# Layer 3 top-32 attention: the last replacing pass of one head of two is given up, and the kept keys of that head are marked by ranks that TensorE counts and ScalarE takes

## The chip, the cores and the metric

One Trainium2 chip, one of its cores. The metric is the device time of one launch in microseconds, the median of the runs. In the views PE is TensorE, DVE is VectorE, ACT is ScalarE, POOL is GpSimd.

## The reference, cut to what matters

The kernel computes a four-layer decoder on 8 sequences of 256 tokens with 128 features. The change is in the attention of layer 3, with a smaller edit in that of layer 2. Layer 3 has 16 heads of 8 features, and each query keeps only its 32 largest scores (`K = 32`):

```python
def _L3_attn_ref(x, Wq, bq, Wk, bk, Wv, bv, Wo, bo):
    ...
        top_s, top_i = jax.lax.top_k(scores, kk)
    ...
```

The scores are `q k^T / sqrt(8)` (256 by 256 per head and sequence), the kept ones go through a softmax, all others count as nothing, and the result is mixed with the values and projected by `Wo`. Of equal scores at the border the one at the lower position is kept.

## The kernel before

**The stage.** `topk_attention` works on 64 groups (`GROUPS`). A group is two heads of one sequence, cut in four units (`U = 4`) of 128 queries by 256 keys: units 0 and 1 are the first head, units 2 and 3 the second. The scores of a group fill two PSUM banks, and group n + 2 uses those of group n. Each engine runs an order written out by hand, a loop over t, and waits on semaphores that count.

- `score` (PE, L3719): four FP32 matmuls with 32 rows (a head is padded to 32), the two heads at two different row groups of the array. It waits until ScalarE has read the banks (`probs_ready` of group n - 2).
- `choose` (DVE, L3885 and L3888): four rounds. A round is four MAX8 (eight largest of each query) and four MATCH_REPLACE8 (puts -3e38 in their places in `raw`). After round four the 32 largest are gone from `raw`. The last instruction gives `scores_max`.
- `soften` (ACT, L3821 to L3829): the negated maximum as bias, the sum over the 32 kept ones (`few`), then for each unit the exponential of all scores (`probs`) and that of `raw` (`rest`).
- `pick` (POOL, L3936, L3938): `probs - rest` leaves the kept ones; then times the inverse of the sum.
- `turn` (PE, L3765): eight FP32 transposes; `take_turned` (ACT, L3838) copies them out of PSUM; `mix` (PE, L3742) multiplies with the values.
- On even t PE also runs `project` (L3706, L3707: keys and queries of the next tile, which is two groups), and ACT takes them in `take_queries` (L3811, L3812). On odd t ACT takes the mixed heads in `take_heads` (L3846), which waits for `mix`. Every eighth group `put_out` multiplies with `Wo`. In the first 16 steps keys and values of the next sublayer are made in between (`project_context`).

So in step t ScalarE softens group t - 1 and then copies the turned group t - 2, while VectorE works on group t.

**The layer 2 stage.** `delta_outputs` has 16 units. For each, PE makes the scores of four bands of 32 rows (L2670, L2673) in four banks, DVE multiplies all of them by a mask in one instruction (L2749, 1536 columns) and PE mixes (L2688, L2691). The banks are single, so the scores of a unit wait for the mask of the one ahead.

Of the kernel before, what the change touches and what calls it, by code (L numbers as in the profile page):

```python
# [11 lines left out]
ALU = mybir.AluOpType  # L12
# [2609 lines left out]
def delta_outputs(c, k, q_odd, q_even, U, padded, masks, probs, oT, inv_q, gates, vt, o_t, squares, sums):  # L2622
# [27 lines left out]
    with nc.Block() as block:  # L2650
        @block.tensor
        def _(pe):
# [11 lines left out]
            def score(n):  # L2664
                b, e = units[n]
                src = (q_even, q_odd)[e]
                if n >= 1:
                    pe.wait_ge(c.scores_masked.sem, c.scores_masked.at(n))
                for j in range(4):
                    nc.tensor.matmul(scores(j)[:, 0:3:2, :], k[band[j], b * S:b * S + P], src[band[j], b * S:(b + 1) * S],  # L2670
                                     start=True, stop=True, tile_position=(32 * j, 0))
                for j in range(4):
                    mm = nc.tensor.matmul(scores(j)[:, 1, :], k[band[j], b * S + P:(b + 1) * S],  # L2673
                                          src[band[j], b * S + P:(b + 1) * S], start=True, stop=True,
                                          tile_position=(32 * j, 0))
                mm.then_inc(c.scores_ready.sem, 1)

            def mix(n):
                b, e = units[n]
                pe.wait_ge(c.scores_masked.sem, c.scores_masked.at(n + 1))  # L2680
# [60 lines left out]
        def _(dve):  # L2741
            v = nc.vector
            for n in range(len(units) + 5):
                if n < len(units):
                    b, e = units[n]
                    dve.wait_ge(c.scores_ready.sem, c.scores_ready.at(n + 1))
                    if n >= 2:
                        dve.wait_ge(c.mixed_ready.sem, c.mixed_ready.at(n - 1))
                    v.tensor_tensor(probs[n % 2], c.psum[:, 0:4, 0:3 * P].rearrange("p j (a x) -> p j a x", x=P),  # L2749
                                    masks[:, b % 4].unsqueeze(1).broadcast_to([P, 4, 3, P]), ALU.mult) \  # L2750
                        .then_inc(c.scores_masked.sem, 1)
# [20 lines left out]
    for s, n in ((c.updates_moved, 4), (c.updates_placed, 4), (c.scores_ready, len(units)), (c.scores_masked, len(units)),  # L2772
# [878 lines left out]
def topk_attention(c):  # L3651
# [6 lines left out]
    NG, GROUPS, TILES = H // 2, B * H // 2, B * H // 4  # L3658
    a = Arena(c)
# [6 lines left out]
    top8, few = a.take(2, U, K // 8, 8), a.take(2, U, K)  # L3666
    values = c.T[:, 0, :].rearrange("p (t f) -> p t f", f=P)
# [11 lines left out]
    def held(tile):  # L3679
        return bank(6)[:, tile % 2 * S:(tile % 2 + 1) * S]  # L3680
# [14 lines left out]
    with nc.Block() as block:  # L3695
        @block.tensor
        def _(pe):
# [12 lines left out]
            def score(n):  # L3710
                tile = n // 2
                if n % 2 == 0:
                    pe.wait_ge(c.qk_taken.sem, c.qk_taken.at(tile + 1))
                if n >= 2:
# [921 lines left out]
```

## Time and profile before

| | |
|---|---|
| runs | 2515.19 us median of 3 (2509.85 to 2515.55) |
| profiled execution | 2510.24 us, span 2508.4 us |
| busy share of the span | PE 75%, DVE 69%, ACT 45%, POOL 28% |
| mean granted clock of PE | 0.812 of full speed |
| layer 3 attention stage | about 1526 to 2296 us of the span |

### The profile page before, as it was taken

How to read it: one execution, taken by the hardware profiler on the slowest of the kernel's cores; microseconds unless marked ns; L12 is line 12 of the kernel's file. 1: busy time of each engine (PE TensorE's matmuls, PEld its weight loads, DVE VectorE, ACT ScalarE, POOL GpSimd, SP SyncE). 2: the span in 40 equal slices, each digit the busy share in tenths (PEclk: the TensorE clock that was granted, in tenths of full speed). 3: DMA queues.
4: the chain of work that ended last, by engine and by line, in shares of the span. 5: the costliest groups of instructions: out<-in, count | busy, mean ns of one | idle time of the engine just before them, and what ended most of it. 6: DMA issues, size and time to landing. Idle time of an engine off the chain costs nothing. (4 is left out here: it accounts for less than half of the span.)

```text
span 2508.4 us, 36866 instructions
## 1 busy us (share of the span) xinstructions
PE 1871.5 (75%) x11751; PEld 1113.4 (44%) x11763; DVE 1736.4 (69%) x5543; ACT 1134.2 (45%) x3143; POOL 711.7 (28%) x620
## 2 busy tenths in 40 slices
PE   6996889853877999979997875565555555555778
PEld 2654447442445666644464553343333333333443
DVE  4236342267765666657746777999999999995655
ACT  3653442251315777731233654555555555454411
POOL 1200045014432333310032411444433433332130
PEclk8997899965998999989998896666666566566979
DMA  5000001400000000000200000000000000000000
GB/s 212 2 1 1 27 27 29 151 14 1 2 2 1 2 2 1 0 1 0 94 2 1 1 1 1 1 1 1 1 1 1 1 1 1 1 1 1 1 1 17
DMA packets 10591, 37.76 MB, mean 15 GB/s; under 512 B 1344, under 2 KB 7488, under 8 KB 9136
## 3 DMA queue, kind: packets, MB, share of 16 engines
q1 hardware_dynamic: 8880, 33.04, 3.4%
q0 software_dynamic: 1536, 2.59, 0.4%
q8 instruction: 85, 1.39, 0.2%
q14 instruction: 90, 0.74, 0.1%
HBM read 30.15 MB, written 5.51 MB: 14 GB/s over the span
## 5 line engine op out<-in xcount | busy, mean ns | idle before, releaser
L3719 PE MATMUL psum<-work 32*128 32x256 f32 x512 | 130.5, 654 | 291.8 <-ACT work L3829 291.8
L3888 DVE MATCH_REPLACE8 work<-work 128x256 f32<-128x256 f32 x768 | 304.8, 405 | 0.0
L3936 POOL TENSOR_TENSOR work<-work 128x1024 f32<-128x1024 f32 x64 | 150.6, 2354 | 494.5 <-ACT work L3829 494.5
L3885 DVE MAX8 work<-work 128x8 f32<-128x256 f32 x768 | 266.1, 406 | 0.0
L3719 PEld LDWEIGHTS psum<-work 32*128 32x128 f32 x512 | 77.6, 311 | 318.2 <-ACT work L3829 161.8
L709 POOL TENSOR_TENSOR work<-work 128x256 f32<-128x256 f32 (+2 forms) x144 | 133.3, 944 | 225.9 <-DVE work L997 225.9
L925 ACT ACTIVATE work<-work 128x128 f32<-128x128 f32 (+1 forms) x320 | 144.9, 454 | 19.1 <-DVE work L972 17.3
L3829 ACT ACTIVATE work<-work 128x256 f32<-128x256 f32 x256 | 128.4, 502 | 0.0
L3742 PE MATMUL psum<-work,tiles 128*8 128x256 f32 x512 | 117.2, 610 | 13.6 <-ACT work L3838 13.6
L3938 POOL TENSOR_TENSOR work<-work 128x1024 f32<-128x1024 f32 x64 | 121.1, 1892 | 6.2 <-DVE work L3910 1.2
L3827 ACT ACTIVATE work<-psum,work 128x256 f32<-128x256 f32 x256 | 117.4, 459 | 0.0
L3765 PE MATMUL psum<-small_weights,work 128*128 128x128 f32 x512 | 100.8, 362 | 15.6 <-POOL work L3938 15.6
L3765 PEld LDWEIGHTS psum<-small_weights,work 128*128 128x128 f32 x512 | 83.5, 191 | 61.9 <-POOL work L3938 42.5
L352 DVE RECIPROCAL work<-work 128x128 f32<-128x128 f32 x36 | 34.3, 952 | 107.2 <-ACT work L424 106.9
L3888 DVE MATCH_REPLACE8 work<-work,psum 128x256 f32<-128x256 f32 x256 | 102.8, 411 | 0.0
L966 DVE CUSTOM_DVE_ANT_0 work<-psum,work 128x128 f32<-128x128 f32 (+1 forms) x320 | 99.6, 367 | 2.8
L3885 DVE MAX8 work<-psum 128x8 f32<-128x256 f32 x256 | 90.5, 413 | 7.7 <-PE psum L3719 5.8
L891 ACT ACTIVATE work<-psum,big_weights 128x256 f32<-128x256 f32 x128 | 57.9, 473 | 76.3 <-PE psum L773 75.7
L2209 DVE TENSOR_TENSOR work<-work,psum 128x320 f32<-128x320 f32 (+1 forms) x56 | 32.0, 573 | 74.7 <-PE psum L2047 66.0
L1285 ACT ACTIVATE work<-psum 128x1024 f32<-128x1024 f32 x64 | 62.0, 1021 | 42.2 <-PE psum L1192 42.2
L273 PE MATMUL psum<-residual,small_weights 128*128 128x512 f32 x96 | 56.4, 719 | 31.7 <-PEq L169 17.8
L3823 ACT ACTIVATE work<-work 128x32 f32<-128x32 f32 x256 | 79.0, 310 | 2.1
(616 smaller groups left out, 4629.3 us busy)
## 6 DMA issues: line engine op xcount, KB each, us to landing
big_weights<-L0f_dram SPq DMA_DIRECT2D x1, 6117.5 KB, 29.3
big_weights<-L_dram SPq DMA_DIRECT2D x1, 5772.0 KB, 17.5
big_weights<-L_dram SPq DMA_DIRECT2D x1, 4952.5 KB, 15.8
choice_rows<-tiles SPq DMA_DIRECT2D x2, 1024.0 KB, 10.5
tiles<-choice_rows SPq DMA_DIRECT2D x8, 256.0 KB, 5.0
big_weights<-L_dram SPq DMA_DIRECT2D x1, 2027.0 KB, 20.2
big_weights<-L_dram SPq DMA_DIRECT2D x1, 1630.5 KB, 13.8
big_weights<-L0f_dram SPq DMA_DIRECT2D x1, 1630.5 KB, 6.4
```

The lines of the kernel that those rows point to most:

```text
L709: ins = nc.gpsimd.tensor_tensor(part, part, rsum[:, g % 4, q:U:U // n].unsqueeze(2) .broadcast_to([P, n, seen(q)]), ALU.mult)
L925: ins = nc.scalar.activation(probs[:, g % 2, u, 0:seen(u)], src, ACT.Exp, bias=nbias[:, g % 2, u:u + 1], scale=scale, accum_out=sums[:, g ...
L966: ins = nc.vector.tensor_tensor_reduce(raw[:, s, u, 0:seen(u)], scores(g)[:, u, 0:seen(u)], mask(mb, u % 2)[:, 0:seen(u)], 1.0, NEG, ALU.a ...
L3719: mm = nc.tensor.matmul(scores(n)[:, u, :], qb[head, tile % 2, u % 2 * P:(u % 2 + 1) * P], kb[head, tile % 2, :], start=True, stop=True, t ...
L3742: mm = nc.tensor.matmul(held(tile)[at:at + D, :], values[:, 2 * b + kt, lo:lo + D], turned[:, n % 2, head, kt, :], start=(kt == 0), stop=( ...
L3765: mm = nc.tensor.transpose(bank(4 + head)[:, at:at + P], probs[:, n % 2, 2 * head + q, kt * P:(kt + 1) * P], ident)
L3827: nc.scalar.activation(probs[:, s, u, :], scores(n)[:, u, :], ACT.Exp, bias=nbias[:, s, u:u + 1], scale=SCALE)
L3829: ins = nc.scalar.activation(rest[:, s, u, :], raw[:, s, u, :], ACT.Exp, bias=nbias[:, s, u:u + 1], scale=SCALE)
L3885: ch.step(v.max(top8[:, n % 2, u, r, :], src[:, u, :]))
L3888: ins = v.match_replace(raw[:, n % 2, u, :], top8[:, n % 2, u, r, :], src[:, u, :], REPLACED)
L3936: ch.link(g.tensor_tensor(mine, mine, rest[:, n % 2], ALU.subtract))
L3938: g.tensor_tensor(mine, mine, rsum[:, n % 2, :].unsqueeze(2).broadcast_to([P, U, S]), ALU.mult) \
```

## The change

For each group but the last (`FINAL` = 63) the units 2 and 3 (`M = 2`, one head) are marked in another way:

- VectorE leaves out the last two MATCH_REPLACE8 of round four.
- ScalarE writes `sign(threshold - score)` of these units as bf16, with a sum (`balance`), ahead of `few`; it leaves out two exponentials of `raw`. Then it squares the turned signs (`square`), and takes the ranks from PSUM (`keep_ranks`), and only then copies the turned probabilities of the group in front.
- TensorE turns the signs (`turn_signs`), and adds up seven bf16 matmuls in the score banks of units 2 and 3 (`rank`). The score matmuls of group t + 1 come in two halves: head one ahead of `rank`, head two behind it (and behind `project`), since its banks must have been read by `keep_ranks`.
- GpSimd subtracts 512 columns instead of 1024, clamps the ranks between 0 and 1 and multiplies units 2 and 3 by them.
- `held` has one buffer instead of two (the other half of bank 6 holds the turned signs).

The last group keeps the old marking, but VectorE does the subtraction and the scaling unit by unit, copies one of the two turned heads, and adds the last output itself; three quarters of the last `put_out` go ahead, and ScalarE copies the turned group 62 ahead of softening group 63. In `delta_outputs` scores and mask go in halves of two bands.

```diff
@@ delta_outputs
-                for j in range(4):
-                    nc.tensor.matmul(scores(j)[:, 0:3:2, :], k[band[j], b * S:b * S + P], src[band[j], b * S:(b + 1) * S],
...
+                for half in range(2):
+                    if n >= 1:
+                        pe.wait_ge(c.scores_masked.sem, c.scores_masked.at(2 * n - 1 + half))
+                    for j in (2 * half, 2 * half + 1):
...
@@ topk_attention, tensor
+            def turn_signs(n):
+                pe.wait_ge(signs_ready.sem, signs_ready.at(n + 1))
...
+                for kt in range(2):
+                    for u in range(M):
+                        mm = nc.tensor.transpose(signs_t[:, kt, u, :], signs_by_unit[:, u, kt * P:(kt + 1) * P], ident16)
+                mm.then_inc(signs_turned.sem, 1)
+
+            def rank(n):
+                pe.wait_ge(squares_kept.sem, squares_kept.at(n + 1))
+                order = scores(n)[:, U - M:U, :]
+                nc.tensor.matmul(order.rearrange("p u k -> p (u k)"), far, signs, start=True, stop=False)
+                for u in range(M):
+                    nc.tensor.matmul(order[:, u, :], one_row[0:1, :], place_row[0:1, :], start=False, stop=False)
+                    for kt in range(2):
+                        mm = nc.tensor.matmul(order[:, u, :], squares[:, kt, u, :], prefix[:, kt, :], start=False,
+                                              stop=(kt == 1 and u == M - 1))
+                mm.then_inc(ranks_ready.sem, 1)
...
             for t in range(GROUPS + 3):
+                if 0 <= t - 1 < FINAL:
+                    turn_signs(t - 1)
                 if t + 1 < GROUPS:
-                    score(t + 1)
+                    score(t + 1, 0, U - M)
+                if 0 <= t - 1 < FINAL:
+                    rank(t - 1)
                 if t % 2 == 0 and t // 2 + 1 < TILES:
                     project(t // 2 + 1)
+                if t + 1 < GROUPS:
+                    score(t + 1, U - M, U)
...
@@ topk_attention, scalar
+                    signed = nc.scalar.activation(signs_by_unit[:, m, :], scores(n)[:, u, :], ACT.Sign, scale=-1.0,
+                                                  bias=top8[:, s, u, LAST, 7:8], accum_out=balance[:, s, m:m + 1])
...
+            def square(n):
+                act.wait_ge(signs_turned.sem, signs_turned.at(n + 1))
...
+            def keep_ranks(n):
+                act.wait_ge(ranks_ready.sem, ranks_ready.at(n + 1))
...
+                for u in range(M):
+                    ins = nc.scalar.activation(ranks[:, u, :], scores(n)[:, U - M + u, :], ACT.Relu, scale=2.0,
+                                               bias=balance[:, n % 2, u:u + 1])
+                ins.then_inc(ranks_kept.sem, 1)
...
+                if t == GROUPS:
+                    take_turned(t - 2)
                 if 0 <= t - 1 < GROUPS:
                     soften(t - 1)
-                if 0 <= t - 2 < GROUPS:
+                if 0 <= t - 1 < FINAL:
+                    square(t - 1)
+                if 0 <= t - 1 < FINAL:
+                    keep_ranks(t - 1)
+                if 0 <= t - 2 < GROUPS and t != GROUPS:
                     take_turned(t - 2)
...
@@ topk_attention, vector
+                replaced = U - M if r == LAST and n < FINAL else U
...
-                for u in range(U):
+                for u in range(replaced):
...
@@ topk_attention, gpsimd
-                ch.link(g.tensor_tensor(mine, mine, rest[:, n % 2], ALU.subtract))
+                ch.link(g.tensor_tensor(first, first, rest[:, n % 2, 0:U - M], ALU.subtract))
+                pool.wait_ge(ranks_kept.sem, ranks_kept.at(n + 1))
+                ch.link(g.tensor_scalar(ranks, ranks, 1.0, 0.0, ALU.min, ALU.max))
+                ch.link(g.tensor_tensor(marked, marked, ranks, ALU.mult))
```

TensorE's order, one even step in the middle of the stage (the semaphores in brackets are what the first of a row waits for). Before:

```order
L3765 MATMUL psum<-small_weights,work 128x128 [waits turned_copied,probs_picked]
L3765 MATMUL psum<-small_weights,work 128x128 x7
L3719 MATMUL psum<-work 128x256 [waits probs_ready]
L3719 MATMUL psum<-work 128x256 x3
L3706 MATMUL psum<-normed_input,big_weights 128x256 [waits qk_taken]
L3707 MATMUL psum<-normed_input,big_weights 128x256
L3742 MATMUL psum<-work,tiles 8x256 [waits out_copied,turned_copied]
L3742 MATMUL psum<-work,tiles 8x256 x3
```

The same step in the changed kernel (`aux_s` is `signs_ready`, `aux_s2` is `squares_kept`, `aux_s3` is `ranks_kept`):

```order
L3806 MATMUL psum<-small_weights,work 128x128 x7
L3747 MATMUL psum<-work 128x128 [waits aux_s]
L3747 MATMUL psum<-work 128x128 x3
L3735 MATMUL psum<-work 128x256 [waits probs_ready]
L3735 MATMUL psum<-work 128x256
L3753 MATMUL psum<-work 128x512 [waits aux_s2]
L3755 MATMUL psum<-work 128x256
L3757 MATMUL psum<-work 128x256 x2
L3720 MATMUL psum<-normed_input,big_weights 128x256 [waits qk_taken]
L3721 MATMUL psum<-normed_input,big_weights 128x256
L3735 MATMUL psum<-work 128x256 [waits aux_s3]
L3782 MATMUL psum<-work,tiles 8x256 [waits out_copied,turned_copied]
```

The four score matmuls no longer stand together: seven rank matmuls (L3753, and L3755 with two L3757 twice), the projection and a wait for ScalarE stand between the first head and the second.

ScalarE's order in an odd step, before and then in the changed kernel (`aux_pe` is `signs_turned`, `aux_pe2` is `ranks_ready`):

```order
L3827 ACTIVATE work<-psum,work 128x256
L3829 ACTIVATE work<-work 128x256
L3838 COPY work<-psum 128x512 [waits mixed_ready,probs_turned]
L3838 COPY work<-psum 128x512
L3821 ACTIVATE work<-work 128x4 [waits probs_turned,sums_inverted,scores_max]
```

```order
L3873 ACTIVATE work<-work 128x4 [waits probs_turned,sums_inverted,scores_max]
L3877 ACTIVATE work<-psum,work 128x256 x2
L3883 ACTIVATE work<-work 128x32 x3
L3887 ACTIVATE work<-psum,work 128x256 x4
L3892 ACTIVATE work<-work 128x256 x2
L3899 ACTIVATE work<-psum 128x512 [waits aux_pe]
L3908 ACTIVATE work<-psum,work 128x256 [waits probs_picked,aux_s,aux_pe2]
L3917 COPY work<-psum 128x512 [waits mixed_ready,probs_turned]
L3925 COPY work<-psum 128x256 [waits mixed_ready]
```

Between the exponentials and the copy of the turned probabilities ScalarE now has two places at which it waits for TensorE (L3899, L3908), and everything behind them waits too.

## Rows read from the trace of the kernel before

**Rows 1.** Windows: the attention stage, then two stretches of one group.

```profile
core 0: us, PE busy (x) PEld busy (x) DVE busy (x) ACT busy (x) POOL busy (x), PEclk, DMA share, GB/s
1526.00:2276.00 750.00, 429.79 (x1754) 243.31 (x1750) 747.01 (x3138) 393.00 (x1304) 286.53 (x145) 0.63 0.00 1
1908.10:1915.20 7.10, 7.10 (x26) 4.04 (x27) 7.10 (x32) 1.73 (x4) 4.25 (x2) 0.50 0.00 1
1915.20:1918.60 3.40, 0.42 (x4) 0.18 (x2) 3.40 (x15) 3.20 (x14) 0.00 (x0) 1.00 0.00 0
```

**Rows 2.** Two waits of the stage: total, times, longest.

```profile
PE psum L3719 <- ACT work L3829: 291.8, 62, 6.4
...
DVE work L3885 <- PE psum L3719: 5.8, 1, 5.8
```

**Rows 3.** Timeline of one group: start, time, engine, line.

```profile
1903.45 0.21 ACT L3821 ACTIVATE work<-work 128x4 f32<-128x4 f32 x1 [2.57 <-DVE work L3888]
1903.62 1.42 DVE L3885 MAX8 work<-psum 128x8 f32<-128x256 f32 x4 [0.20 <-DVE work L3888]
...
1904.92 0.45 ACT L3827 ACTIVATE work<-psum,work 128x256 f32<-128x256 f32 x1
...
1905.02 0.41 DVE L3888 MATCH_REPLACE8 work<-work,psum 128x256 f32<-128x256 f32 x1
1905.28 0.50 ACT L3829 ACTIVATE work<-work 128x256 f32<-128x256 f32 x1
...
1905.42 0.41 DVE L3888 MATCH_REPLACE8 work<-work,psum 128x256 f32<-128x256 f32 x1
...
1907.94 1.06 ACT L3838 COPY work<-psum 128x512 f32<-128x512 f32 x2
...
1908.10 2.08 PE L3719 MATMUL psum<-work 32*128 32x256 f32 x8 [5.25 <-ACT work L3829]
...
1910.11 1.22 PE L3706 MATMUL psum<-normed_input,big_weights 128*128 128x256 f32 x2
1910.56 1.89 POOL L3938 TENSOR_TENSOR work<-work 128x1024 f32<-128x1024 f32 x1
...
1912.12 1.88 PE L3742 MATMUL psum<-work,tiles 128*8 128x256 f32 x8
1912.22 0.47 ACT L3811 ACTIVATE work<-psum,big_weights 128x256 f32<-128x256 f32 x1 [3.23 <-PE psum L3707]
...
1915.25 1.08 DVE L3885 MAX8 work<-psum 128x8 f32<-128x256 f32 x3
```

**Rows 4.** Source view of L288: two row groups together, then one alone.

```profile
L288 PE MATMUL psum<-work,small_weights x8: 270/270/372, 1515.5 to 1516.0; 32*128 32x128 f32 x8
...
L288 PE MATMUL psum<-work,small_weights x4: 270/270/372, 1516.7 to 1517.2; 32*128 32x128 f32 x4
```

**Rows 5.** Nearest rows for added operations, grouped by form.

```profile
L4333 PE MATMUL psum<-work,small_weights 128*128 128x512 bf16 x30 | 11.2, 380 | 1.2 <-PEq L1575 1.2
...
L3954 POOL TENSOR_TENSOR tiles<-tiles,big_weights 128x512 f32<-128x512 f32 x4 | 5.1, 1270 | 0.3
...
L3166 POOL TENSOR_SCALAR tiles<-tiles 128x2048 f32<-128x2048 f32 x1 | 2.2, 2212 | 0.1
```

**Rows 6.** Timeline of two units of the layer 2 stage.

```profile
727.43 0.71 PE L2670 MATMUL psum<-tiles 32*128 32x256 f32 x8 [0.72 <-DVE work L2749]
...
728.44 1.76 DVE L2749 TENSOR_TENSOR tiles<-psum,work 128x1536 f32<-128x1536 f32 x1 [0.73 <-PE psum L2673]
...
730.25 0.71 PE L2670 MATMUL psum<-tiles 32*128 32x256 f32 x8 [1.09 <-DVE tiles L2749]
```

**Rows 7.** Timeline of the end of the attention stage.

```profile
2276.66 0.21 ACT L3821 ACTIVATE work<-work 128x4 f32<-128x4 f32 x1 [3.72 <-DVE work L3888]
...
2285.72 1.97 PE L3765 MATMUL psum<-small_weights,work 128*128 128x128 f32 x8 [1.57 <-POOL work L3938]
...
2295.19 0.72 POOL L3944 TENSOR_TENSOR residual<-residual,work 128x256 f32<-128x256 f32 x1 [9.53 <-remote]
```

More of the change, by code:

```diff
@@ L3666, in topk_attention @@
     top8, few = a.take(2, U, K // 8, 8), a.take(2, U, K)
+    M, LAST = U // 2, K // 8 - 1
+    signs, squares = (a.take(M * S // 2).bitcast(BF16) for _ in range(2))
+    signs_by_unit = signs.rearrange("p (u k) -> p u k", u=M)
+    squares = squares.rearrange("p (t u q) -> p t u q", t=2, u=M)
+    ranks, balance = a.take(M, S), a.take(2, M)
+    ident16, far, place_row, one_row = (a.take(n // 2).bitcast(BF16) for n in (P, P, S, P))
+    prefix = a.take(2, S // 2).bitcast(BF16)
+    strict = a.take(P)
+    signs_ready, signs_turned, squares_kept, ranks_ready, ranks_kept = c.aux_s, c.aux_pe, c.aux_s2, c.aux_pe2, c.aux_s3
     values = c.T[:, 0, :].rearrange("p (t f) -> p t f", f=P)
@@ L3708, in project, with score @@
                     .then_inc(c.qk_ready.sem, 1)
-            def score(n):
+            def score(n, lo_unit, hi_unit):
                 tile = n // 2
-                if n % 2 == 0:
+                if n % 2 == 0 and lo_unit == 0:
                     pe.wait_ge(c.qk_taken.sem, c.qk_taken.at(tile + 1))
-                if n >= 2:
+                if n >= 2 and lo_unit == 0:
                     pe.wait_ge(c.probs_ready.sem, c.probs_ready.at(n - 1))
-                for u in range(U):
+                if n >= 2 and hi_unit == U:
+                    pe.wait_ge(ranks_kept.sem, ranks_kept.at(n - 1))
+                for u in range(lo_unit, hi_unit):
                     lo = (n % 2 * 2 + u // 2) * 32
@@ L3766, in turn @@
                                                      probs[:, n % 2, 2 * head + q, kt * P:(kt + 1) * P], ident)
+                    if n == FINAL and head == 0:
+                        mm.then_inc(c.probs_turned.sem, 1)
+                        pe.wait_ge(c.probs_picked.sem, c.probs_picked.at(n + 2))
                 mm.then_inc(c.probs_turned.sem, 1)
@@ L3783, in _ @@
             make_values(0)
-            score(0)
+            score(0, 0, U)
             make_values(1)
@@ L3836, in take_turned @@
                     act.wait_ge(c.mixed_ready.sem, c.mixed_ready.at(n - 1))
-                for head in range(2):
+                for head in range(1 if n == FINAL else 2):
                     ins = nc.scalar.copy(turned[:, n % 2, head].rearrange("p t s -> p (t s)"), bank(4 + head))
@@ L3954, in mask_context, with tables @@
                     ch.link(g.tensor_tensor(x, x, c.w("L3x_vmask").unsqueeze(1).broadcast_to([P, CH // P, P]), ALU.mult))
-            for t in range(GROUPS + 4):
-                if 0 <= t - 1 < GROUPS:
+            def tables():
+                g.tensor_copy(ident16, ident)
+                g.tensor_scalar(far, ident, -512.0, 0.0, ALU.mult, ALU.add)
+                g.tensor_scalar(place_row, c.w("position"), -1.0, float(K), ALU.mult, ALU.add)
+                g.memset(one_row, 1.0)
+                g.memset(prefix[:, 0, P:], 0.5)
+                g.memset(prefix[:, 1, 0:P], -0.5)
+                ch.link(g.tensor_tensor(strict, c.w("upper"), ident, ALU.subtract))
+                ch.step(g.tensor_scalar(prefix[:, 0, 0:P], strict, 1.0, -0.5, ALU.mult, ALU.add))
+                ch.link(g.tensor_scalar(prefix[:, 1, P:], strict, 1.0, -0.5, ALU.mult, ALU.add))
+                g.memset(strict, 0.0).then_inc(c.tables_ready.sem, 1)
+            tables()
+            for t in range(GROUPS + 3):
+                if 0 <= t - 1 < FINAL:
                     pick(t - 1)
```

114 lines of the change are left out of this document (79 added, 35 removed).

## The prediction

> **What bounds the kernel now.** I first read the windows of the attention stage [rows 1]. It holds 750 of the 2508 us of the span, and VectorE is busy for 747.0 of them. PE is busy for 430 us at a mean granted clock of 0.63, ScalarE for 393, GpSimd for 287. The waits say the same: PE waits 291.8 us for ScalarE's last exponential in 62 places, which costs nothing, while VectorE waits for scores once, 5.8 us at the start [rows 2]. Then I read the timeline of one group [rows 3]. VectorE starts it at 1903.62 and the next one at 1915.25, so a group takes 11.63 us. ScalarE begins to soften at 1903.45, 0.03 us after VectorE's last record. PE gets the score banks at 1908.10 and has the new scores in them 2.08 us later, at 1910.18, more than 5 us before VectorE asks for them at 1915.25. The stage is VectorE's alone, and whatever shortens a group there shortens the stage, as long as the circle from VectorE through ScalarE and PE back to VectorE, and ScalarE's own row of work, stay under the new length of a group.
>
> **What is removed.** Two MATCH_REPLACE8 in 63 groups. They start 0.40 apart (1905.02, 1905.42), a little less on the mean of a round, so I take 0.395 each [rows 3]. A group of VectorE becomes 11.63 - 0.79 = 10.84 us. 63 x 0.79 = 50 us is the ceiling of this part.
>
> **What is added on ScalarE.** Offsets are from the start of softening. The bias copy and the four sums take 1.47 us (1903.45 to 1904.92). An exponential from PSUM starts 0.36 before its neighbour (1904.92 to 1905.28); all eight take 3.02 (to 1907.94), which leaves 0.395 for one from SBUF [rows 3]. Sign with a sum isn't in the trace: at least 0.36, at most the 0.45 of the record and a read of the sum behind it, some 0.65. A sum of 32 columns costs 0.31 ((1.47 - 0.24)/4), about 0.1 over a plain one, so I take 0.46, and 0.92 for both, of which the wait behind the bias copy hides 0.1. Sums end at 2.3, four exponentials at 3.75, two at 4.55, with the last record's tail `probs_ready` comes at 4.65. Before, it came at 4.65 too (1908.10). The square is a 512-column read of PSUM like the copies (1.06 for two): 0.53, done at 5.1, behind the score matmuls and so hidden.
>
> **What is added on PE, and the price of cutting the scores in two.** Rank is 2048 columns of bf16 (512 and six times 256). The nearest row is 512 columns in 380 ns at full clock, 11.2 us busy for 30 [rows 5]. Some 0.17 of it is the way of the last column through the array, and 0.21 its own; at half clock I take 0.43, so rank is 1.7 plus 0.16 for the first weights and 0.2 for the last column, 2.07 us; at full clock about 1.05. If bf16 cost what FP32 does (0.5 for a record of 256 columns, half of the 2.01 us from 1910.11 to 1912.12 over two records each [rows 3]), it would be 4. The four transposes of signs are 512 columns, 0.6 or 0.35.
>
> The part that the diff hides is `score`. L288 multiplies FP32 with 32 rows in one row group of the array. Eight records at two row groups stand between 1515.5 and 1516.0, and four records at one row group between 1516.7 and 1517.2, with the same durations [rows 4]. So two row groups run side by side, and half the matmuls at one row group take as long. The scores before have exactly this form, two heads at two row groups, 8 records in 2.08 us. Cut by head, each half takes the whole 2.0 us at half clock (1.0 at full), and PE pays the scores twice: +2.0 per group, and 1.0 of it stands ahead of rank, where it would otherwise be.
> The Trainium skill, TensorEngine Tiling, "Theoretical Speedup", allows up to 4x for a contraction of 32 rows, one array tile beside the other. By it a lone head could use a quarter of the array, and the trace agrees in kind: two tiles gave 2x, and one gives nothing. Without such packing the cut would cost nothing, and the sums below would be 1.0 us shorter at each half.
>
> **At which clock.** PE is granted 0.50 for the 7.10 us in which it is busy without a gap, and 1.00 for the 3.40 us behind, when it has almost nothing to do [rows 1]. The mean of 0.63 is 74% of the time at half speed. So I work the step out for both.
>
> Half clock, even step: `probs_ready` 4.65; first head 4.70 to 6.71; rank to 8.8; ScalarE takes the ranks, 0.82 for two (0.36 and a record of 0.46), to 9.7; the copy of the turned group, 1.06, to 10.7. PE projects from 8.6 to 10.7, ScalarE takes the queries, 0.85 (1912.22, two records of 0.47 overlapping), to 11.6. Second head 10.6 to 12.7, mix 1.88 [rows 3] to 14.5, turn 1.97 [rows 7] to 16.5, signs of the next group 17.0; they should be there at 4.65 of the next step, 16.3: 0.7 late.
> Odd step: ranks taken 9.7, copy 10.7, second head 9.7 to 11.7, mix to 13.6, and the heads are taken behind it, 0.4 (256 columns from PSUM, like an exponential): 14.0.
> A pair takes 11.6 + 0.7 + 14.0 = 26.3 us, 13.15 per group, bound by ScalarE that waits for PE.
> Full clock: first head 5.7, rank 6.8, ranks taken 7.6, copy 8.7; even: queries 9.6; odd: second head 8.7, mix 9.8, heads 10.2. Both are under 10.84, and VectorE stays the bound.
>
> The new loop through GpSimd is near that too: ranks taken, clamp, two multiplications (1.27 for 512 columns [rows 5], 1.89 for 1024 [rows 3]), turn, signs, first head, rank, ranks. The clamp isn't there; GpSimd's only comparable row is 2.21 for 2048 columns [rows 5], a quarter of it 0.55, so between 0.55 and 2.21, and I take 0.66. With 0.2 for the three links this is 4.0 + 2.0 + 0.5 + 2.0 + 2.1 + 0.9 = 11.5 at half clock and 8.5 at full.
>
> **The sum.** What stays open is the mix of the clocks. PE gets more to do (7.1 us of work per step become some 11.5 at half clock), which speaks for more time at full speed than now; but two heads one after the other fill less of the array, and 7.10 us of gapless work weren't enough before. I take 65% at half: 10.84 + 0.65 x (13.15 - 10.84) = 12.34, that is +0.71 against 11.63, and 63 x 0.71 = +45 us.
> The tail: from 2276.66 to the last GpSimd record's end at 2295.91 are 19.25 us [rows 7]. After: softening starts 2 to 4 us later, because the turned group 62 is copied first; then 4.6 to the last exponential, 1.3 for VectorE's last two pieces, 1.0 for four transposes, 0.6 copy, 1.9 mix, 0.4 heads, 0.7 for one product of four, 0.45 for the addition: 13 to 15. So -5.
> `delta_outputs`: a unit takes 2.82 us (727.43 to 730.25), 1.01 for scores and 1.76 for the mask [rows 6]. Its scores run at four row groups at once, so half of them takes as long as all, and PE's work per unit becomes 0.9 + 0.9 + 0.8 for the mix + 0.2 = 2.8 less what the halves still overlap; VectorE's floor is about 2.2. Between 0 and -0.6 for 16 units, I take -0.2: -3.
> Total +45 - 5 - 3 = +37 on the profiled execution's own 2510.2, 2547. That execution lies 5 us under the median of 2515.2 and beside the lowest run, so I put the median after at 2550.
>
> **The rivals.**
> 1. *VectorE stays the bound (faster).* If PE is at full speed nearly all through the stage, each group is 10.84: -50 - 5 - 3 = -58, 2455. For it: PE would be busy in almost every stretch of a half-clock step, and the stretches of pauseless work get longer. It decides at the share of half clock where 10.84 + s x 2.31 = 11.63 + 8/63, s = 0.40; below that the kernel is faster. Against it: at full clock PE pauses from about 2.3 to 4.7 of each step. The Trainium skill, TensorE: Matmul & The Clock Gate, "What's actually happening", says that sustained work brings 2.4 GHz and idleness 1.2; [rows 1] shows the rise only at 1915.20, when the step's work was over. Chance 0.20.
> 2. *PE stays at half clock.* 13.15 per group, +96 - 8 = +88, 2600 and a little more, if the clamp is at its upper bound too. Chance 0.17.
> 3. *The two balance,* near s = 0.40, no difference: 0.08. A mild gain between it and the first: 0.05.
> 4. The forecast, a mix: 0.50.
>
> **How the numbers follow.** Slower 0.67 (4 and 2), within 0.3% 0.08, faster 0.25; 0.3% is about 8 us, roughly what this measurement can tell. The range leaves out the lower half of the first rival's cases and the far end of the second: 2462 to 2618. The forecast's own range is 2522 to 2588 (s from 0.45 to 0.9).
>
> **What would show it.** The two halves of `score` at 2.0 us each at clock 0.50; VectorE idle ahead of its first MAX8 of a group, released by PE's second half, or ScalarE's softening later than 0.03 us behind VectorE's last record; ScalarE waiting at L3899 and L3908 for some 3 us a group. It is wrong if VectorE is busy for nearly all of the stage after too, or if the halves of `score` take 1 us at half clock, or if PE is granted over 0.85 in the mean.

## The result and the profile after

The changed kernel takes 2582.28 us (median of 4 runs, 2581.62 to 2599.37) against 2515.37 for the kernel before: a ratio of 1.0293 (95% interval 1.0274 to 1.0312), 2.9% slower. The medians alone give 1.027; the ratio weighs all executions, 2599.4 us among them, but that of experiment e4 leaves out its slow one, 2605.6 us. The direction was forecast, the size was not: by medians +35 us forecast, +67 measured.

The page of the kernel after, busy time by engine, over its profiled span of 2580.0 us:

```profile
PE 2094.7 (81%) x12412; PEld 1231.4 (48%) x12456; DVE 1696.7 (66%) x5317; ACT 1212.2 (47%) x3456; POOL 759.2 (29%) x753
```

Its windows view of the attention stage, columns as in [rows 1], and the waits of that stretch (engine and line, released by; total, times, longest, in us):

```profile
1526.00:2330.00 804.00, 628.31 (x2319) 346.74 (x2349) 675.49 (x2776) 457.54 (x1569) 325.23 (x266) 0.64 0.00 1
```

```profile
POOL work L4038 <- ACT work L3892: 260.5, 58, 12.6
POOL work L4040 <- ACT work L3908: 207.8, 61, 4.4
ACT work L3908 <- PE psum L3757: 187.2, 61, 4.0
DVE work L3971 <- PE psum L3735: 114.2, 43, 5.2
PE psum L3735 <- ACT work L3892: 101.1, 40, 3.1
...
ACT work L3925 <- PE psum L3782: 76.7, 29, 3.0
```

VectorE, busy 747 of 750 us before [rows 1], is now busy 675 of 804 and stands 114 us ahead of its first MAX8, released by the second part of the scores; before that was 5.8 us, once [rows 2]. PE went from 430 us of 750 to 628 of 804, at the same mean clock, 0.64 for 0.63.

The stage's first and last group, by VectorE's first MAX8:

```profile
1522.92 0.76 DVE L3971 MAX8 work<-psum 128x8 f32<-128x256 f32 x2 [6.15 <-PE psum L3735]
...
2344.42 0.76 DVE L3971 MAX8 work<-psum 128x8 f32<-128x256 f32 x2 [1.91 <-PE psum L3735]
```

821.5 us for 63 groups; the same two starts in the trace before lie 738.3 apart. So the span's +71.6 us (2508.4 to 2580.0) are: +83.2 in the groups, -3.7 ahead of them, -5.8 in the tail up to the next stage's first matmul, and -2.1 behind. Ahead of them lies `delta_outputs`: from its first score matmul to the end of its last mask it takes 40.7 us for 45.9. Everything that went wrong is in the groups. Two steps of them, PE and ScalarE alone, even step first:

```profile
1903.50 2.07 PE L3735 MATMUL psum<-work 32*128 32x256 f32 x4 [2.34 <-ACT work L3892]
1905.51 0.61 PE L3753 MATMUL psum<-work 128*128 128x512 bf16 x1
...
1907.62 1.06 PE L3720 MATMUL psum<-normed_input,big_weights 128*128 128x256 f32 x2
1907.87 0.84 ACT L3908 ACTIVATE work<-psum,work 128x256 f32<-128x256 f32 x2 [3.94 <-PE psum L3757]
...
1909.47 2.07 PE L3735 MATMUL psum<-work 32*128 32x256 f32 x4
1910.30 0.21 ACT L3873 ACTIVATE work<-work 128x4 f32<-128x4 f32 x1
1911.47 1.88 PE L3782 MATMUL psum<-work,tiles 128*8 128x256 f32 x8
...
1915.46 1.12 PE L3735 MATMUL psum<-work 32*128 32x256 f32 x4
...
1918.90 2.07 PE L3735 MATMUL psum<-work 32*128 32x256 f32 x4 [0.93 <-ACT work L3908]
```

Each head's scores, x4 records, take 2.07 us at clock 0.50; before, both heads, x8, took 2.08 [rows 3]. Of these parts the one at 1915.46 alone is at full speed (1.12). ScalarE stands 3.94 us for the ranks. And once in eight groups there is a step that the forecast has no sum for:

```profile
1880.29 1.88 PE L3782 MATMUL psum<-work,tiles 128*8 128x256 f32 x8
1882.10 3.16 PE L3791 MATMUL psum<-work,big_weights 128*128 128x256 f32 x8
1885.10 1.04 PE L3806 MATMUL psum<-small_weights,work 128*128 128x128 f32 x8
...
1885.30 0.47 ACT L3931 ACTIVATE work<-psum,big_weights 128x256 f32<-128x256 f32 x1 [6.07 <-PE psum L3791]
1885.68 0.20 ACT L3873 ACTIVATE work<-work 128x4 f32<-128x4 f32 x1
...
1890.38 1.11 PE L3735 MATMUL psum<-work 32*128 32x256 f32 x4 [3.14 <-ACT work L3892]
...
1894.68 2.07 PE L3735 MATMUL psum<-work 32*128 32x256 f32 x4 [0.93 <-ACT work L3908]
```

```profile
1896.79 1.09 DVE L3971 MAX8 work<-psum 128x8 f32<-128x256 f32 x3 [3.63 <-PE psum L3735]
```

ScalarE stands 6.07 us for the output product (L3931). The softening behind it starts at 1885.68, PE stands 3.14 us for it, and VectorE gets its next scores at 1896.79, 16.4 us after the last ones. Seven groups have such a step, every eighth from the 12th on: the first takes 16.5 us, the other six 16.4 each.

### The profile page after: what moved, and what is told of

Its sections match the earlier page's. It is cut to its first block and busy times, and to the rows that moved or that the text cites. A ratio compares the mean times of both kernels' runs of the same rounds, so it can differ in the third digit from the quotient of the medians.

```text
span 2580.0 us, 38569 instructions
## 1 busy us (share of the span) xinstructions
PE 2094.7 (81%) x12412; PEld 1231.4 (48%) x12456; DVE 1696.7 (66%) x5317; ACT 1212.2 (47%) x3456; POOL 759.2 (29%) x753
## 5 line engine op out<-in xcount | busy, mean ns | idle before, releaser
L3735 PE MATMUL psum<-work 32*128 32x256 f32 x512 | 216.5, 566 | 133.1 <-ACT work L3892 103.4
L3974 DVE MATCH_REPLACE8 work<-work 128x256 f32<-128x256 f32 x642 | 255.5, 407 | 0.0
L3735 PEld LDWEIGHTS psum<-work 32*128 32x128 f32 x512 | 122.1, 265 | 194.1 <-ACT work L3892 85.0
L4038 POOL TENSOR_TENSOR work<-work 128x512 f32<-128x512 f32 x63 | 79.8, 1267 | 266.9 <-ACT work L3892 266.7
L3908 ACT ACTIVATE work<-psum,work 128x256 f32<-128x256 f32 x126 | 52.8, 470 | 192.7 <-PE psum L3757 192.7
L3806 PE MATMUL psum<-small_weights,work 128*128 128x128 f32 x512 | 111.8, 391 | 25.8 <-POOL work L4043 24.2
L3806 PEld LDWEIGHTS psum<-small_weights,work 128*128 128x128 f32 x512 | 92.3, 207 | 70.2 <-POOL work L4043 65.0
L4043 POOL TENSOR_TENSOR work<-work 128x1024 f32<-128x1024 f32 x63 | 119.2, 1892 | 4.9
L3782 PE MATMUL psum<-work,tiles 128*8 128x256 f32 x512 | 109.5, 575 | 3.9 <-ACT work L3917 3.1
L4040 POOL TENSOR_SCALAR work<-work 128x512 f32<-128x512 f32 x63 | 38.6, 612 | 214.8 <-ACT work L3908 214.8
L3887 ACT ACTIVATE work<-psum,work 128x256 f32<-128x256 f32 x256 | 99.6, 477 | 0.0
L4041 POOL TENSOR_TENSOR work<-work 128x512 f32<-128x512 f32 x63 | 79.8, 1266 | 5.3
```

The source lines that it names most:

```text
L3735: mm = nc.tensor.matmul(scores(n)[:, u, :], qb[head, tile % 2, u % 2 * P:(u % 2 + 1) * P], kb[head, tile % 2, :], start=True, stop=True, t ...
L3782: mm = nc.tensor.matmul(held[at:at + D, :], values[:, 2 * b + kt, lo:lo + D], turned[:, n % 2, head, kt, :], start=(kt == 0), stop=(kt == ...
L3806: mm = nc.tensor.transpose(bank(4 + head)[:, at:at + P], probs[:, n % 2, 2 * head + q, kt * P:(kt + 1) * P], ident)
L3887: nc.scalar.activation(probs[:, s, u, :], scores(n)[:, u, :], ACT.Exp, bias=nbias[:, s, u:u + 1], scale=SCALE)
L3974: ins = v.match_replace(raw[:, n % 2, u, :], top8[:, n % 2, u, r, :], src[:, u, :], REPLACED)
L4038: ch.link(g.tensor_tensor(first, first, rest[:, n % 2, 0:U - M], ALU.subtract))
```

## Experiments

Every ratio is to the kernel before, run on the same chip. That kernel's median was 2515.4 us beside the kernel after, 2516.3 for e1 to e4, 2522.8 for e5 to e8, 2522.9 for e9 to e12 and 2514.2 for e13 and e14, so between these sets the ratios are to be compared and not the times; a difference of 0.0100 is 25 us. Group lengths are from VectorE's first MAX8 to the next group's, the mean of 62 without the first. The clock is the windows view's PEclk over 1560 to 2200 us, with PE's busy time in these 640 us. For the kernel before that is 373 us at 0.64, with groups of 11.66.

| kernel | us | ratio (95%) | group | PE busy | PEclk |
|---|---|---|---|---|---|
| after | 2582.3 | 1.0293 (1.0274 to 1.0312) | 13.02 | 502 | 0.65 |
| e1 no ranks | 2503.4 | 0.9942 (0.9920 to 0.9964) | 11.66 | 371 | 0.63 |
| e8 two less | 2459.4 | 0.9757 (0.9719 to 0.9794) | 10.87 | 395 | 0.64 |
| e2 whole scores | 2536.4 | 1.0081 (1.0053 to 1.0110) | 12.11 | 453 | 0.67 |
| e3 side by side | 2505.8 | 0.9957 (0.9933 to 0.9981) | 11.60 | 445 | 0.68 |
| e6 copy first | 2593.2 | 1.0295 (1.0237 to 1.0353) | 13.11 | 507 | 0.64 |
| e4 output later | 2574.5 | 1.0220 (1.0188 to 1.0253) | 12.68 | 511 | 0.65 |
| e5 three edits | 2494.6 | 0.9898 (0.9864 to 0.9933) | 11.36 | 435 | 0.71 |
| e7 filler | 2473.7 | 0.9816 (0.9775 to 0.9857) | 11.08 | 475 | 0.82 |
| e9 three + filler | 2471.2 | 0.9802 (0.9772 to 0.9833) | 10.95 | 473 | 0.81 |
| e10 filler, after | 2563.9 | 1.0172 (1.0141 to 1.0202) | 12.48 | 537 | 0.74 |
| e11 filler, before | 2518.9 | 0.9991 (0.9975 to 1.0008) | 11.66 | 406 | 0.72 |
| e12 short extras | 2580.7 | 1.0235 (1.0202 to 1.0267) | 12.78 | 517 | 0.61 |
| e13 output last | 2556.8 | 1.0171 (1.0137 to 1.0205) | 12.46 | 519 | 0.64 |
| e14 all last | 2465.7 | 0.9810 (0.9793 to 0.9827) | 10.92 | 477 | 0.82 |

**The parts priced alone.** e1 is the kernel after with the marking by ranks undone:

```
-                    score(t + 1, 0, U - M)
+                    score(t + 1, 0, U)
-                if 0 <= t - 1 < FINAL:
-                    rank(t - 1)
...
-                replaced = U - M if r == LAST and n < FINAL else U
+                replaced = U
```

> The tail and the halved units of delta_outputs as in the kernel after, the attention groups as in the kernel before (all 16 MATCH_REPLACE8, scores in one piece, no signs and no ranks). My forecast priced these two edits at -5 and -3 us. Theory: the whole loss is in the groups, so this is 8 to 9.5 us under the kernel before, 2506 us, and the groups take 11.67 us again. Rival: the edits around the groups hold a part of the loss that the two traces hide from each other; then the time is 2515 us or more.

e8 is e1 with the `replaced` line of the kernel after.

> The kernel without ranks (tail and delta units as after, scores in one piece, 2503.4 us), with the last two MATCH_REPLACE8 of a group left out and nothing in their place: the second head of each group keeps its 25th to 32nd largest in what is subtracted, so its probabilities are not the reference's. It prices the removal alone. Forecast: 63 x 0.79 = 50 us, groups of 10.84 us, 2454 us. Rival: the chain through ScalarE and PE doesn't fit into 10.84 us at half clock even without ranks, and groups end at 11.2 or more, 2475 us.

e1 gave 2503.4, groups of 11.66: the loss lies in the marking alone, and the edits around it bring 9 to 20 us by the interval, where the traces of before and after show 9.5 and the forecast had 8. e8 gave 2459.4; it leaves the second head's marking unfinished, so it is a price and no kernel to use. The two MATCH_REPLACE8 are worth 0.0185, 47 us, and 0.79 us a group, as forecast. Without ranks the chain fits into the shorter group at a mean clock of 0.64.

**The cut of the scores.** e2 puts the scores back in one piece, behind rank:

```
-                if t + 1 < GROUPS:
-                    score(t + 1, 0, U - M)
                 if 0 <= t - 1 < FINAL:
                     rank(t - 1)
...
-                    score(t + 1, U - M, U)
+                    score(t + 1, 0, U)
```

> The kernel after, with the four score matmuls of a group in one piece behind the rank matmuls (and behind the projection in even steps), so that the two row groups run side by side again. Theory A (the cut costs PE the scores twice, half of it ahead of the rank matmuls): rank starts up to 2.0 us earlier in a step, the scores take 2.08 us where the second half took 2.07, and a group gets 0.8 us shorter on the mean, 12.2 us, some 2530 us. The group that takes 16.4 us once in eight stays. Rival B (the cut is cheap, the chain through GpSimd and the late turned copy hold the step): no change that can be told, 2575 to 2585 us, VectorE still idle 114 us before its first MAX8.

e3 keeps the cut but makes it across the heads, one half of the queries of both in each piece:

```
+    def slot(u):
+        return 2 * (u % 2) + u // 2
...
-                    lo = (n % 2 * 2 + u // 2) * 32
+                    lo = (n % 2 * 2 + u % 2) * 32
...
-                    mm = nc.tensor.matmul(scores(n)[:, u, :], qb[head, tile % 2, u % 2 * P:(u % 2 + 1) * P],
+                    mm = nc.tensor.matmul(scores(n)[:, slot(u), :], qb[head, tile % 2, u // 2 * P:(u // 2 + 1) * P],
...
-                order = scores(n)[:, U - M:U, :]
-                nc.tensor.matmul(order.rearrange("p u k -> p (u k)"), far, signs, start=True, stop=False)
                 for u in range(M):
-                    nc.tensor.matmul(order[:, u, :], one_row[0:1, :], place_row[0:1, :], start=False, stop=False)
+                    own = scores(n)[:, slot(U - M + u), :]
+                    nc.tensor.matmul(own, far, signs_by_unit[:, u, :], start=True, stop=False)
+                    nc.tensor.matmul(own, one_row, place_row, start=False, stop=False)
...
```

> The kernel after, with another cut: each piece of the scores holds one half of the queries of both heads, so its two matmuls lie in different row groups and different banks. The marked units are the second halves of the queries. The first rank matmul becomes two of 256 columns, and the one of one row has 128 rows of which 127 are zero. Theory A (what costs is that a piece has one row group): a piece takes 1.05 us at half clock instead of 2.07; with one piece ahead of rank and one behind, a group gets up to 2 us shorter where PE bounds it, to about 11.8 on the mean, some 2505 us. Rival B (the chain through GpSimd and ScalarE's order hold the step): 0.3 us per group at most, 2560 us. Rival C (with fewer busy columns the clock stays at 0.50 longer): the pieces get short but the mean clock falls under 0.62 and the time stays over 2530 us.

By ratios e2 takes 53 us off the kernel after and e3 85, or 35 and 66 off e4 below, which has the same order of instructions as the kernel after. Both are as theory A had them, and rival B is out; so is e3's rival C, with a mean clock of 0.68. e3's timeline, two pieces at half clock and full:

```profile
1909.64 1.22 PE L3738 MATMUL psum<-work 32*128 32x256 f32 x4 [2.03 <-ACT work L3894]
...
1914.28 0.70 PE L3738 MATMUL psum<-work 32*128 32x256 f32 x4
```

The same x4 records with the same columns take 1.22 where the kernel after pays 2.07. e3 gives back about all of the 67 us that the kernel after lost, though it changes two other things with the cut: the first rank matmul comes in two, and the one of one row has 128 rows. e2 changes nothing but the cut and the place of the scores. The Trainium skill, TensorEngine Tiling (Array Packing), "Theoretical Speedup", gives up to 4x for a dimension of 32. The traces bear out that there is something to gain, and show a condition that decides here: a piece must hold work for more than one row group. In e3 the two matmuls of a piece start 0.01 us apart, in the kernel after one follows the other. They need not alternate in the code: the kernel before gives both matmuls of one head and then both of the other, and the four take 2.08 us [rows 3].

**ScalarE's order.** e6 and e4 each change one thing in ScalarE's program of the kernel after, e5 changes both in e3:

```
+                if 0 <= t - 2 < GROUPS and t != GROUPS:
+                    take_turned(t - 2)
                 if 0 <= t - 1 < FINAL:
                     keep_ranks(t - 1)
-                if 0 <= t - 2 < GROUPS and t != GROUPS:
-                    take_turned(t - 2)
```

> The kernel after with one move on ScalarE: the copies of the turned probabilities go ahead of the ranks. In the kernel after, ScalarE stands 3.1 us at the ranks in each step. Theory A (the cut scores make PE the bound, it has no gap behind the rank matmuls in even steps): at half clock the copy ends before rank does, so ranks are kept at the same time and the mix is no longer behind the copy; but PE takes up the second piece as before and a group changes by under 0.3 us: 2565 to 2585 us. Rival B (ScalarE's order costs the time): at least 0.8 us per group less, 2530 us or lower.

```
             for t in range(GROUPS + 4):
+                if t >= 11 and (t - 11) % NG == 0 and t < GROUPS + 3:
+                    take_output((t - 11) // NG)
...
-                if t >= 10 and (t - 10) % NG == 0 and t < GROUPS + 2:
-                    take_output((t - 10) // NG)
```

> The kernel after, with ScalarE's taking of the output product moved from the end of its step to the start of the next one. Theory: the group of 16.4 us once in eight comes from ScalarE standing at that wait (up to 6.3 us) while the next softening is due; without it these groups take 13 us, 7 x 3.4 = 24 us less, some 2557 us. Rival: PE is late in these steps by the product itself, and ScalarE waits elsewhere for the same time: the groups of 16 us stay and the time is 2575 us or more.

> The kernel with pieces of the scores side by side (2505.8 us), and two moves on ScalarE as well: the turned probabilities of the group in front are copied ahead of the ranks, and the output product is taken at the start of the next step. In that kernel a group takes 11.6 us on the mean against a floor of 10.84, 14 of 62 are over 12, and once in eight it is 13.2. Theory A (what is left is ScalarE standing at the ranks, 2.5 us a group, with the copy and so the mix behind it): the copy goes into that wait, groups come to 11.1 on the mean, 2475 us. Rival B (what is left is PE at the half clock, whatever ScalarE's order): ranks come later by the copy's 1.0 us, the second piece with them, and the time stays between 2495 and 2510 us.

e6: no difference from the kernel after (1.0295 and 1.0293). Although ScalarE stands 187 us at the ranks, its order isn't what costs. e4 doesn't do what was meant: between the end of step t and the start of the next one ScalarE has nothing else in those steps, so the order of instructions is the same as in the kernel after on every engine. It says nothing on the product, and is a second measurement of the kernel after's order: 1.0220 (1.0188 to 1.0253) for 1.0293 (1.0274 to 1.0312), 18 us apart. Its trace has 800.4 us for the 63 groups, for 821.5. The two traces agree within 0.1 us a group up to the 12th; from the 36th on e4's groups with the product take 14.4 us for 16.4. Windows of one such group, in the kernel after and in e4:

```profile
2085.26:2101.64 16.38, 11.14 (x44) 6.20 (x43) 11.02 (x45) 7.21 (x25) 4.36 (x4) 0.71 0.01 2
```

```profile
2077.44:2091.85 14.41, 9.17 (x44) 5.29 (x43) 10.93 (x45) 7.22 (x25) 5.38 (x5) 0.81 0.01 2
```

The same 44 instructions of PE, at 0.81 for 0.71, are busy 2 us less. Whether the build, the chip or the execution decides which of the two rhythms a run falls into isn't shown. Below, less than 0.0073 (18 us) between two kernels with PE as the bound is not read as an effect. e5, which so is e3 with the copy first, lies 15 us under e3 by ratios (11 by medians), within that bound and nearer to rival B.

**The clock.** e7 is e3 with work whose product nobody reads:

```
+            def fill():
+                for _ in range(10):
+                    nc.tensor.matmul(bank(4)[:, 0:S], ident16, prefix[:, 0, :], start=True, stop=True)
...
+                if 2 <= t <= FINAL:
+                    fill()
                 if 0 <= t - 1 < GROUPS:
                     turn(t - 1)
```

> The kernel with pieces of the scores side by side (2505.8 us), and 10 bf16 matmuls of 256 columns whose product nobody reads, ahead of the transposes of each step, where PE stands some 2 us for GpSimd. They take 1.1 us at full clock and 2.1 us at half. Theory A (the granted clock sets what is left over the floor, and it follows what PE does): PE's mean clock in the stage rises from 0.68 to over 0.75 and the time falls below 2495 us. Rival B: the clock doesn't move, the matmuls are paid at half clock where PE has no gap, and the time rises to 2515 us or more.

e10 puts the same lines into the kernel after, e9 into e5; e11 puts two FP32 matmuls in that place into the kernel before.

> The kernel after, unchanged but for the 10 matmuls that nobody reads ahead of the transposes of each step. Here PE has only 0.0 to 0.2 us ahead of its transposes at half clock. Theory A (the half clock is the larger part of the price of the cut): the mean clock of the stage rises from 0.64 to over 0.72 and the time falls under 2550 us although they cost 1.1 to 2.1 us a step. Rival B (PE has no room in these steps at either clock): each step at half clock gets 2 us longer, 2620 us or more.

> The kernel before with two FP32 matmuls of 256 columns whose product nobody reads (0.5 us each at full clock, 1.0 at half) ahead of the transposes of each step. It tells whether such matmuls bring anything where PE isn't the bound. Theory: VectorE has every score 4 us early, so the groups stay at 11.63 us and the time at 2515 us, whatever the clock does. Rival: they help by another way than the waits for PE, and the time falls under 2505 us as it fell in the kernel with pieces side by side.

> The kernel with the three edits (pieces side by side, turned copy ahead of the ranks, output product taken a step later: 2494.6 us) and the 10 matmuls that nobody reads ahead of the transposes of each step. Theory A (order and clock are two separate causes of what is left over the floor of 10.84): groups come to 10.9 on the mean, 2462 us, as good as the two MATCH_REPLACE8 left out without any replacement. Rival B (the ten matmuls already took what the order would give): 2470 to 2478 us, the time with them alone (2473.7).

Windows 1560 to 2200 us, in this order: e3, e7 and e10 (columns as in [rows 1]):

```profile
1560.00:2200.00 640.00, 445.49 (x2186) 259.29 (x2184) 600.59 (x2481) 410.66 (x1416) 295.62 (x238) 0.68 0.00 1
```

```profile
1560.00:2200.00 640.00, 475.28 (x2863) 289.19 (x2863) 627.39 (x2598) 431.58 (x1488) 310.23 (x250) 0.82 0.00 1
```

```profile
1560.00:2200.00 640.00, 536.54 (x2465) 306.46 (x2466) 559.88 (x2309) 380.38 (x1310) 275.28 (x222) 0.74 0.00 1
```

e7 takes 35 us off e3 by ratios. PE has 677 instructions more in these 640 us, the clock goes from 0.68 to 0.82, and all its other work gets so much shorter that its busy time rises by 30 us only. Theory A holds. In the kernel after (e10) the clock rises too, from 0.65 to 0.74, but by ratios the time falls by 30 us against the kernel after and by 12 against e4, whose interval it overlaps, so a gain isn't sure. It is neither theory's number. PE is busy 537 us for 502, so the likely reason, not shown by a run of its own, is that the ten matmuls take a part of what the clock gives. In e11, with two FP32 matmuls for the ten, the clock is 0.72 for 0.64 and the time the same: here, where VectorE is the bound, the higher clock brought nothing. e9 isn't told apart from e7 (rival B); with the clock up, ScalarE's order is worth nothing that can be told.

**PE's occasional work.** e12 shortens it in the kernel after:

```
-                for j in range(lo, hi):
+                for j in ((3,) if hi == 4 else ()):
...
-                    mm = nc.tensor.matmul(bank(7), c.w("L3x_wk"), c.CT[:, n * CH:(n + 1) * CH], start=True, stop=True)
+                    mm = nc.tensor.matmul(bank(7)[:, 0:64], c.w("L3x_wk"), c.CT[:, n * CH:n * CH + 64], start=True, stop=True)
...
```

> The kernel after with PE's occasional work in the stage cut down: of the output product once in eight steps only the last of four matmuls is done, and of the 512 columns of each piece of context that early odd steps project only 64, so the outputs are not the reference's. My step sums left both out. Theory A (they are what the sum of the forecast missed): the groups of 16.4 us and the early ones of 15 to 17 come down to 13, and the time to about 2550 us. Rival B (the plain steps were mis-sized, by the clock's share or by a late chain): 2570 us or more.

No gain that can be told: 1.0235, between e4's 1.0220 and the kernel after's 1.0293. Its window:

```profile
1560.00:2200.00 640.00, 517.40 (x1869) 277.34 (x1869) 543.84 (x2243) 373.54 (x1278) 268.42 (x217) 0.61 0.00 1
```

PE has less to do, is granted 0.61 for 0.65, and is busy longer, 517 us for 502. The groups with the product are 15.4 for 16.4, those of the early pieces of context 12.6 for 13.3, and the other 40 are no shorter (12.4 for 12.3). The time is rival B's, but it doesn't show that the rare steps cost nothing: with the work, clock went too. e13 keeps the work and moves it:

```
-                if t >= 10 and (t - 10) % NG == 0:
-                    put_out((t - 10) // NG, 3 if t == GROUPS + 2 else 0, 4)
...
                     turn(t - 1)
+                if 10 <= t < GROUPS and (t - 10) % NG == 0:
+                    put_out((t - 10) // NG, 0, 4)
```

with `take_output` on ScalarE at the end of step t + 1 (a real move, unlike e4's). e14 is e9 with the same.

> The kernel after with the whole output product moved behind the transposes of its step on PE, and its taking on ScalarE to the end of the next step, so that neither the transposes of group t-1 nor the softening of group t stand behind it. Theory A (the order makes the group of 16.4 us): these groups take 13 us, 7 x 3.4 = 24 us less, some 2557 us, at the same clock. Rival B (PE is full in these steps wherever the product stands, or the clock gives less): the length goes over into the next group, and the time stays over 2572 us.

> The kernel with the three edits and the 10 matmuls that nobody reads (2471.2 us, groups of 10.95 us on the mean), with the output product behind the transposes as well. There only 11.2 to 11.8 us in one group of eight are left to gain, some 0.5 us seven times: Theory A: 2465 to 2471 us. Rival B: it makes no difference at all or the later taking delays a projection, 2471 us or more.

The product in e13's timeline, with the transposes ahead of it, and what follows:

```profile
1888.41 1.97 PE L3806 MATMUL psum<-small_weights,work 128*128 128x128 f32 x8
1890.17 2.16 PE L3791 MATMUL psum<-work,big_weights 128*128 128x256 f32 x8
1892.17 0.39 PE L3747 MATMUL psum<-work 128*128 128x128 bf16 x4
```

2556.8, theory A's 2557. By ratios it is 31 us under the kernel after and 12 under e4, whose interval it overlaps, so the time alone doesn't show the gain against both. The trace does: the groups of 16.4 are gone (10.8 to 11.4 in those places), and the 40 plain groups behind the 17th are as they were (12.28 for 12.34), at the mean clock of the kernel after (0.64). The 63 groups take 786.9 us, for 821.5 and e4's 800.4. e14 isn't told apart from e9 and e7 by its ratio.

## Why the prediction was right in direction and wrong in size

**Removed work:** right. 0.79 us a group, 50 us in the groups of e8 against e1 (688.2 for 738.0).

**Cut of the scores:** right, shown by the trace (2.07 us each at 0.50), by e2 and by e3, where the cut across the heads gives 66 to 85 us back. The signs that were named came as well: VectorE waits for PE's second half (114 us), and ScalarE stands some 3 us a group at L3908.

**Added durations:** near. Clamp 0.61 (0.66 forecast), square 0.61 (0.53), two signs with their reads of the sum 0.44 apart, 1885.78 to 1886.22 (0.46), the first two by form in the view of lines:

```profile
L4040 POOL TENSOR_SCALAR work<-work 128x512 f32<-128x512 f32 x63 | 38.6, 612 | 214.8 <-ACT work L3908 214.8
L3899 ACT ACTIVATE work<-psum 128x512 bf16<-128x512 bf16 x63 | 38.1, 605 | 11.9 <-PE psum L3747 11.9
```

**Tail and `delta_outputs`:** -5.8 and -5.2 against -5 and -3. The first score matmul of `delta_outputs` starts anywhere between 700.9 and 719.0 us in the sixteen traces, so a few us ahead of the groups can't be put down to the edit by the start of the groups.

**The term that was mis-sized is the groups':** +45 forecast, +83 measured. The step that failed is the one from two step sums to 63 groups: the sums covered a plain even and a plain odd step, and put at nothing, without a reason, the one step in eight with the output product and the odd steps among the first 16, which carry a piece of context. The trace of the kernel after by groups (the first takes 14.3 us for 15.1 before):

| groups | mean us | over 12.34 |
|---|---|---|
| 7 with the output product | 16.40 | 28 us |
| the 15 others from the 2nd to the 17th | 13.25 | 14 us |
| the 40 plain ones behind | 12.34 | |

1. *The plain groups* are at the 12.34 of the forecast. Against the kernel before 62 groups of that length and the first one make +41, for the +45.
2. *The output product* stands between mix and transposes, with ScalarE waiting for it ahead of a softening: 28 us. That its place does this is shown by e13's trace, where these groups take 10.95.
3. *The pieces of context* lie in the early groups, 14 us over. That they are the cause is argued: e12 cut them short together with the product.
Together 41 + 28 + 14 = 83.

**Luck in the plain groups.** 12.34 was 10.84 + 0.65 x 2.31. The share of 0.65 was too low: I took a gain of clock because PE would have more to do, but the mean of the stage is 0.64, (1 - 0.64)/0.5 = 72% at half speed, and that of the 40 plain groups 0.63, 75%. With 75% the formula gives 12.56, 0.2 more than they take. So two errors cancelled. The two ends of the mixing are about right: the twelve groups that are at 0.50 throughout take 13.0 us on the mean, for 13.15, and the six at 0.81 or more 11.0, for 10.84.

**The rivals.** A gain needed a share under 0.40. It isn't out of reach: e7, e9 and e14 come to clocks of 0.81 and 0.82, a share of 36 to 38%, with 10.92 to 11.08 us a group. But it takes work made for nothing to get there, and scores that are cut across the heads; the same ten matmuls in the kernel after (e10) reach 0.74 and 12.48. The second rival's 13.15 a group comes near the measured mean of 13.02 for another reason: PE isn't at half clock throughout.

**The rule on the clock** (the Trainium skill, TensorE: Matmul & The Clock Gate, "What's actually happening"): sustained work brings the full clock. e7, e10 and e11 agree in kind: with more work on PE the clock rose. The kernel after doesn't: it is busy without a gap for 11.6 us at 0.50 (below), and 78% of the window at 0.65, against 74% at 0.82 in e7. That more *necessary* work per step would raise the clock was my reading, and these numbers contradict it.

**What stays open.** Why the kernel after gets no more clock than before with a third more busy time isn't settled: no run separates the kind of its work (scores of 32 rows) from the place of its gaps. Nor is why the kernel after and e4, of one order, fall into two rhythms, nor what the pieces of context cost alone.

**The version that beats both** is e14 (2465.7, ratio 0.9810, interval 0.9793 to 0.9827), with e7 and e9 level with it: the pieces of the scores cut across the heads, and 10 short matmuls ahead of the transposes.

## What to carry to other kernels

When matmuls with few contraction rows run beside each other in row groups, cut the work across the groups and not between them: here a piece that fills one group alone cost as much as the whole (2.07 us for 2.08). When an engine has become the bound, write the sums for the rare steps too, since one in eight that puts a wait ahead of the critical activation cost 28 us, more than half of the 50 that were sought. Where a time depends on the clock, measure a second build of the same order before you read a difference of half a per cent. And look whose time a removal takes: 0.79 us off VectorE was paid for with (628 - 430)/63 = 3.1 us of PE's time a group.

## What the runs showed of the hardware

- Less work on PE came with a lower clock: three of four matmuls of the product and most columns of the context pieces gone, and the granted clock was 0.61 for 0.65 (e12), with no time gained that can be told. More of it, read by nobody, came with 0.82 for 0.68 and 35 us less (e7 against e3).
- PE worked 11.6 us without a gap at 0.50 before its clock rose, longer than the 7.1 us of [rows 1]. Windows of the kernel after:

```profile
1903.50:1915.10 11.60, 11.60 (x36) 6.26 (x37) 7.74 (x32) 7.44 (x26) 5.19 (x5) 0.50 0.00 1
1915.10:1918.00 2.90, 2.62 (x15) 1.42 (x14) 2.90 (x14) 0.60 (x1) 1.11 (x1) 0.98 0.00 0
```

- Two kernels with one instruction order lie 18 us apart by ratios where PE is the bound (the kernel after and e4), and their traces differ in where PE gets its full clock.
